# Where the weights of a sorted tile come from: a DRAM row loaded by SyncE instead of a copy by ScalarE

## The reference

```python
x = x + 0.5 * ffn(layernorm(x), Wg, bg, W1, b1, W2, b2)
x = x + attn(layernorm(x))
x = x + 0.5 * ffn(layernorm(x), Wg, bg, W1, b1, W2, b2)

def ffn(x, Wg, bg, W1, b1, W2, b2):          # 8 experts, the best 2 for each token
    probs = softmax(x @ Wg + bg)
    w, idx = top_k(probs, 2);  w = w / sum(w)
    h = relu(x @ W1[e] + b1[e])               # 128 -> 256, each expert e
    y = h @ W2[e] + b2[e]                     # 256 -> 128
    return sum over the two chosen e of w[e] * y[e]

def attn(x):                                  # 16 heads of 8 features
    c = x - mean(x over the tokens)
    return softmax(c @ c.T) @ x               # for each head
```

## Time and profile before

| | |
|---|---|
| median of 3 runs | 1019.24 us (1018.61 to 1019.99) |
| span of the profiled execution | 1039.1 us |
| TensorE busy | 975.9 us, 94% |
| ScalarE busy | 833.7 us, 80% |
| VectorE busy | 789.0 us, 76% |
| GpSimd busy | 529.3 us, 51% |
| ScalarE's `chosen<-weights` | 56 times, 59.2 us |
| DMA | 96.15 MB, mean 93 GB/s |

### The profile page before, as it was taken

How to read it: one execution, slowest core, us unless ns; L and a number is a source line. 1 busy time by engine, 2 the same in 40 slices (tenths; PEclk the granted TensorE clock), 3 DMA queues, 4 the chain that set the end, 5 groups by cost and what they waited for, 6 DMA issues and landing times.

```text
span 1039.1 us, 20329 instructions
## 1 busy us (share of the span) xinstructions
PE 975.9 (94%) x6512; PEld 546.9 (53%) x6512; DVE 789.0 (76%) x2255; ACT 833.7 (80%) x1194; POOL 529.3 (51%) x623
## 2 busy tenths in 40 slices
PE   7899999999999999989999999998999998888995
PEld 5687777633332488843333323332688862246673
DVE  5799999867767789857777777776878754368997
ACT  4655553599999988879999999998999988865653
POOL 5546777744444314354677766666100006555775
PEclk8999999999999999999999999999999999899998
DMA  6444223000051234420111111261444421133443
GB/s 182 165 152 133 100 102 103 14 21 20 19 147 60 75 130 163 145 89 24 36 37 35 36 37 34 57 179 36 122 139 146 143 83 49 44 127 107 131 155 121
DMA packets 59821, 96.15 MB, mean 93 GB/s; under 512 B 9179, under 2 KB 30403, under 8 KB 59715
## 3 DMA queue, kind: packets, MB, share of 16 engines
q1 hardware_dynamic: 47568, 71.50, 21.5%
q0 software_dynamic: 10752, 22.04, 7.1%
q10 hardware_dynamic: 1396, 1.31, 0.4%
HBM read 56.36 MB, written 38.45 MB: 91 GB/s over the span
## 4 chain that ended last, share of the span: by engine, by line
PE 53%; ACT 18%; issue 11%; DVE 10%; POOL 3%; DMA 3%; another core or an unknown queue 1%; SPq 0%; ACTq 0%; POOLq 0%; DVEq 0%
ACT probs L2023 10%; PE ps L1764 10%; PE ps L1749 6%; ACT sums L2023 5%; DVE low L1007 3%; PE ps L1375 3%; PE ps L1377 3%; PE ps L1376 2%; PE ps L1361 2%; PE ps L1386 2%; PE ps L1387 2%; PE ps L1391 2%; PE ps L1398 2%; PE ps L732 2%; PE ps L734 2%
## 5 line engine op out<-in xcount | busy, mean ns | idle before, releaser
L2023 ACT ACTIVATE probs<-ps 128x1024 f32<-128x1024 f32 x344 | 337.1, 1126 | 20.4 <-PE ps L1749 20.0
L1704 POOL DMA_INDIRECT found<-tiles,home x168 | 168.2, 1001 | 198.7 <-ACT sums L2023 126.9
L1692 POOL DMA_INDIRECT sorted<-xn,slot x168 | 168.1, 1000 | 179.2 <-ACT probs L2023 63.0
L1764 PE MATMUL ps<-probs,value 128*32 128x512 f32 x1376 | 185.2, 610 | 3.1 <-ACT probs L2023 1.4
L2023 ACT ACTIVATE sums<-ps 128x1024 f32<-128x1024 f32 x168 | 173.8, 1127 | 7.8 <-PE ps L1749 6.9
L1749 PE MATMUL ps<-shared 32*128 32x512 f16 x1024 | 144.7, 387 | 20.5 <-ACT probs L2023 6.8
L1188 ACT ACTIVATE high<-ps 128x512 fp32r<-128x512 f32 x176 | 101.1, 593 | 74.3 <-PE ps L734 58.7
L1007 DVE SCALAR_TENSOR_TENSOR low<-ps,high 128x512 fp32r<-128x512 f32 x176 | 113.0, 682 | 11.2 <-ACT high L1188 10.2
L1749 PEld LDWEIGHTS ps<-shared 32*128 32x128 f16 x1024 | 37.9, 91 | 157.8 <-ACT probs L2023 72.1
L1264 POOL TENSOR_TENSOR sums<-sums 128x512 f32<-128x512 f32 x59 | 76.6, 1298 | 66.6 <-DVE sums L1039 48.5
L1764 PE MATMUL ps<-sums,value 128*32 128x512 f32 x672 | 90.9, 613 | 0.2 <-ACT sums L2023 0.2
(11 more groups left out here) (202 smaller groups left out, 1869.2 us busy)
## 6 DMA issues: line engine op xcount, KB each, us to landing
found<-sorted SPq DMA_DIRECT2D x56, 256.0 KB
tiles<-sums SPq DMA_DIRECT2D x56, 256.0 KB
probs<-gates SPq DMA_DIRECT2D x24, 512.0 KB
wide<-gates SPq DMA_DIRECT2D x20, 512.0 KB
sorted<-zeros SPq DMA_DIRECT2D x16, 512.0 KB
out<-X SPq DMA_DIRECT2D x15, 256.0 KB
sorted<-xn,slot POOLq DMA_INDIRECT x168
found<-tiles,home POOLq DMA_INDIRECT x168
```

The costliest lines, as they stand in the source:

```text
L1692: nc.gpsimd.indirect_dma_start(sorted_rows[group_of(q)], bass.IndirectOffsetOnAxis(ap=slot[:, q % XNS, k, j:j + 1], axis=0), xn[:, rows_sl ...
L1704: nc.gpsimd.indirect_dma_start(found[:, q % 2, k, j, :], None, tile_rows[group_of(q)], bass.IndirectOffsetOnAxis(ap=home[:, q, k, j:j + 1] ...
L1764: ins = nc.tensor.matmul(ps[q * W:(q + 1) * W, MIX, :], value[:, s % 2, sd, j, m, q, :], ring[ring_at(g * UNITS + 2 * j + q // 2)][:, q % ...
L2023: nc.scalar.activation(ring[ring_at(n)], ps[:, score_banks(n), :], ACT.Exp, scale=SCORE).then_inc(sm["a_probs"], 1)
```

## The change

The split weights are written once to a new DRAM tensor `split` (8 experts x 128 x 1024 values, 4 MB), by one transfer that SyncE issues after the fourth later job's gates (n == 4), once all weights are made. ScalarE's copy `choose` is gone. In its place SyncE reads the number of the tile's expert from `expert_of` into a register and starts a transfer of 512 KB from the expert's row of `split` into the same place of `chosen` (`load_weights`). It waits for the same event as the copy did. `hidden(t)` waits for that transfer. ScalarE still needs the expert's number for the column of the bias, and reads it in `note_expert`, just before `biased`.

```diff
+            def load_weights(t):
+
+                y = tiles_of(t)
+                if t == 0:
+                    sp.wait_ge(sm["split_stored"], 16)
+                if t in TILE0:
+                    sp.wait_ge(sm["g_expert"], y + 1)
+                reached(sp, sm["t_expert"], t - 2)
+                of = nc.sync.value_load(expert_of[0:1, y, tile_at(t):tile_at(t) + 1], min_val=0, max_val=E - 1)
+                sp.dma_start(chosen[:, t % 3, :, :].rearrange("p k f -> p (k f)").bitcast(F32),
+                             split_dram[bass.ds(of, 1), :, :].rearrange("a p c -> p (a c)")).then_inc(weights_in[t % 3], 16)
...
             def sync_stream(a, b, at_slot):
                 for t in range(a, a + 2):
                     load_tile(t)
+                for t in range(a, a + 3):
+                    load_weights(t)
                 for i in stream(a, b):
+                    if i > a and in_stream(i + 2, a, b):
+                        load_weights(i + 2)
                     if in_stream(i + 4, a + 2, b):
                         load_tile(i + 4)
                     if in_stream(i - 2, a, b):
...
+                if n == 4:
+                    sp.dma_start(split_dram.rearrange("e p c -> p e c"),
+                                 weights[:, :, :, :].rearrange("p e k f -> p e (k f)").bitcast(F32)).then_inc(sm["split_stored"], 16)
...
             def hidden(t):
                 u = t % 2
-                pe.wait_ge(sm["t_weights"], t + 1)
+                pe.wait_ge(weights_in[t % 3], 16 * (t // 3 + 1))
...
-            def choose(t):
+            def note_expert(t):
                 if t in TILE0:
                     act.wait_ge(sm["g_expert"], tiles_of(t) + 1)
                 of[t] = nc.scalar.value_load(expert_of[0:1, tiles_of(t), tile_at(t):tile_at(t) + 1], min_val=0, max_val=E - 1)
-                reached(act, sm["t_expert"], t - 2)
-                nc.scalar.activation(chosen[:, t % 3, :, :].rearrange("p k f -> p (k f)"),
-                                     weights[:, bass.ds(of[t], 1), :, :].rearrange("p a k f -> p (a k f)"), ACT.Copy).then_inc(sm["t_weights"], 1)
...
             def biased(t):
+                note_expert(t)
```

More of the change, by code:

```diff
@@ L231, in third, with build @@
     return m % 3 if m < WHOLE * E else (m - WHOLE * E) % 3
-def build(nc, x_in, wg_in, bg_in, w1_rows, b1_in, w2_rows, b2_in, const_in, gates_dram, sorted_rows, tile_rows, out):
+def build(nc, x_in, wg_in, bg_in, w1_rows, b1_in, w2_rows, b2_in, const_in, split_dram, gates_dram, sorted_rows, tile_rows, out):
     with ExitStack() as ctx:
@@ L404, in build @@
         names = """const_in b1_in w1_in_0 w1_in_1 w1_in_2 w1_in_3 w2_in_0 w2_in_1 w2_in_2 w2_in_3 small_in stored value_set set_up wg_set b2_turned b2_set
- w1_shifted w1_high w1_low w2_high w2_low
+ split_stored w1_shifted w1_high w1_low w2_high w2_low
  f_mean f_rstd f_xn f_turned f_xnT f_xh f_xl f_logits f_logit_rows f_logits_turned f_lg f_ahead f_before
@@ L413, in build @@
  g_base g_zrowf g_zrow g_total g_count g_placed g_row g_home g_expert
- t_turned t_xh t_xl t_weights t_hidden t_high t_low t_expert t_y t_back t_out
+ t_turned t_xh t_xl t_hidden t_high t_low t_expert t_y t_back t_out
  c_half c_added
@@ L422, in build @@
         tile_in = sems("tile_in", 4)
+        weights_in = sems("weights_in", 3)
         tile_stored = sems("tile_stored", 2)
@@ L1668, in scalar_stream @@
                     x_high(i + 2)
-                if i == a - 2:
-                    choose(a)
-                    choose(a + 1)
                 if in_stream(i + 1, a, b):
                     relu(i + 1)
[L1674 to L1677, removed]
                 if i == b - 1:
@@ L2295 @@
     tile_rows = [nc.dram_tensor(f"tiles_{y}", ((TILE0[y + 1] - TILE0[y]) * T, D), F32, kind="Internal").ap() for y in range(2)]
-    build(nc, *args, gates_dram, sorted_rows, tile_rows, out)
+    split_dram = nc.dram_tensor("split", (E, P, 4 * F), F32, kind="Internal").ap()
+    build(nc, *args, split_dram, gates_dram, sorted_rows, tile_rows, out)
     return run(nc, [arrays], core_ids=[0]).results[0]["out"]
```

## The result

The changed kernel takes 1050.15 us (median of 4 runs, 1047.18 to 1053.78) against 1019.62 (1018.61 to 1020.1): ratio 1.0294 [1.0265, 1.0324], 30.5 us slower. I had said 1027.5, at most 1045. The direction and the place were right, the size was not.

A forecast was written before the change was run, and what follows sets the result against it. TensorE was taken to bound the kernel; 5.3 (late loads) + 1.5 (second stream's start) + 1.4 (gates) + 0.5 (store) - 0.4 (returns) = 8.3 us, added to 1019.24, gave 1027.5 us (own range 1022 to 1035; overall 1019 to 1045).

The forecast's parts named there:

- what bounds the kernel: Both tile streams: TensorE alone sets the pace, 3.68 us per plain tile, with ScalarE's copies beside it.
- what the copy was worth: Stream starts and last tile: removing ScalarE's copies returns at most 1.2 us, of which 0.4 survives late loads.
- the path: Tile streams: each load stands between tile t-3's expert matmuls and tile t's hidden matmuls, a stretch near 4.33 us.
- step (a): Weight load in the streams: from TensorE's event to the issue on SyncE, register load included, 0.75 us.
- step (b) + (c): Weight load, issue to TensorE: 3.03 us for the first 256 KB plus 0.82 us for 256 KB more.
- L: Total time from TensorE's event until the tile's weights are usable: 4.60 us, with ends 3.78 and 5.03.
- the streams' term: Loads late in both streams: 4.1 us in the second, 1.2 in the first, together 5.3 us; ends 0 and 14.
- Rival C: Streams: DMA engines become the bound, 4.4 to 4.9 us per tile; milder, L reaches 5.5; 1046 us, chance 0.15.
- My sign for it: Profile after, tile streams: a DMA share at 0.95 would show the DMA engines had become the bound.
- The start of the second stream: SyncE's queue: three weight loads ahead of tile load 2 delay the third tile, 1.5 us (0 to 2.5).
- The gates' wait: Mid second stream: SyncE waits for ScalarE's gates, so a weight load goes out 1.5 us late; cost 1.4 us, once.
- The store: Opening, about 117.3 us: the 4.2 MB split-weights store shares the engines with POOL's last send; cost 0.5 us.

## Why the prediction was wrong

**Right: what bounds the kernel and what the copy was worth.** ScalarE's copies lay beside TensorE; 49 us less of ScalarE bought at most the 1.7 to 2.5 us by which both streams together are shorter with four places and early weights. I had 0.4 surviving and 1.2 in all.

**Right: the path.** Expert event, register load, issue, transfer, hidden matmul.

**Half right: step (a), 0.75 us.** It measures 0.73 to 0.79 us in 23 of 50 tiles. In the other 27 it is up to 1.7 (2.07 behind the gates), 0.98 in the mean of all, mostly because the register read itself takes up to 0.99 us in place of 0.26. I had read (a) from one tile load of the kernel before, where no read is longer than 0.39 us. In the tiles that waited, this excess adds up to 6.7 us, so it is at most about a third of the streams' loss.

**Wrong: the transfer, step (b) + (c), 3.85 us.** I took the 3.03 us of tile 0 of the second stream, a load alone in an empty queue, and added only the new load's own second half. The loads of the stream are not alone: each follows a weight load, a tile load and a tile store, 1.05 MB per tile. Issue to landing as the chain has it in the second stream, with the time since the weight load before:

```
issued  751.38  768.32  784.82  794.65  807.04  823.45  840.68
gap       4.20    3.61    3.31    4.30    3.97    3.02    4.00
landed    4.69    5.01    5.60    4.58    5.18    5.47    5.45   us after issue
```

Within the second stream the two go together: 12 loads with a gap of 4.34 us or more landed in 3.2 to 3.8 us, 15 with less in 3.9 to 5.6. The gap is not the whole cause: in the first stream the same groups land in 3.4 to 5.8 and 3.5 to 5.6 us, and the slowest load of all (5.77) had a gap of 4.36. With (a) as it was in these seven tiles, L is 5.7 to 6.8 us for them, against my 4.60 with an upper end of 5.03. The loss per tile is 0.53 us in the second stream (16.0 / 30) instead of 0.15, and the streams' term, 5.3 us in the sum, measures 23.2 - 1.9 = 21.3 us. This is the mis-sized term; it alone is 16 us of the 22.6 by which the measured time is above the forecast. My upper end came from adding bytes to the quiet load. A bound for a queue with a whole tile's 1.05 MB in it would have been, as an estimate, 3.3 to 5.0 us of transfer at the 210 to 318 GB/s of the earlier trace rows, with the rest of the 3.03 us on top (3.03 - 0.262 / 210 = 1.8 us); the slowest landing measured is 5.8. The fit that the prediction quotes from the Trainium skill (DMA: Bandwidth & Descriptors, "Anatomy of one DMA — SWDGE (gpsimd) path") is stated there for GpSimd's transfers, while these loads are issued by SyncE; nothing in the sum hangs on it.

**Rival C was named and put too low.** Its strong form, DMA engines as the bound at 4.4 to 4.9 us per tile, is refuted: 275 GB/s with TensorE never idle. Its mild form, "loads that overlap stretch L to 5.5", is what happened, though not evenly: from the event to the hidden matmul it is 5.5 and 5.4 us in the mean of the two streams, made of tiles at 4.1 and tiles at 7.0. It gave 16 + 8 us in the streams and a total of 1046. I gave all of C 0.15 because I argued the case by throughput (the transfers fit in 3.6 us of 3.68), but traffic that fits, here at a DMA share of 0.79, can still make single loads land too late for a lead of 4.3 us. My sign for it, a share of 0.95, belonged to the strong form.

**The start of the second stream**, 1.5 us: 1.9 by the first three distances, 3.7 in the second trace.

**The gates' wait**, 1.4 us: the delay came and cost nothing. The gates go out at 789.26 and the load behind them at 790.35, 2.1 us after its event, but that tile is not late: the one before had been late already, and its hidden matmul stood at 790.47.

**The store**, 0.5 us: 1.9 by the times (interval 0.1 to 3.9), 0.1 to 1.9 at the send, by the medians 0.6. The argument for it was in part wrong: of the 4.4 us in which the send of the earlier trace rows moved no packet, about 1.6 are not the queue's doing, for a send at 207.18 us in the same trace, with no packet of q1 beside it, moves its first packet after 1.61 us as well.

**The sum by measured terms**, against the span of the kernel with the store alone: 7.2 (first stream) + 16.0 (second, its start included) + 3.5 (behind it) - 0.8 (ahead and between) = 25.9 us; in the second trace of the changed kernel 6.6 + 17.5 + 1.9 - 0.3 = 25.6. What the copies gave back is contained in the lengths. The 3.5 us behind the second stream cannot be put down to the change: that part is 173.8 to 177.6 us long in all traces but the first of before, 176.2 in its second and 176.3 with four places. Nothing is known of the cause of that spread, nor of the 4 us between the two timings of the changed kernel.

No version beats both kernels. The best, 1019.37 us, equals before: in the middle of the second stream TensorE is busy 99.91 of 100 us in before and 100.00 with four places, so there is hardly anything left for a load to give.

## What to carry over

When an on-chip copy is replaced by a load, its price is the lead between the event that frees its buffer and its first reader, against the landing time in the traffic that the stream will then have; a landing read from a quiet moment is a lower end. If all the bytes fit but with little to spare, ask for the data one tile earlier before doing anything about bytes: a place more took 20 to 24 us off here. Leaving out a quarter of the bytes took 20 to 25 where they were half of each late load, and 11 to 15 where they were other loads. Loads whose address is known early go ahead of the loads that wait for data.

## What the hardware showed that I had not expected

- One core's 16 DMA engines held 275 GB/s of mixed loads and stores at a share of 0.85 for 100 us without a late tile, while the single 512 KB loads in this stretch took 3.4 to 5.3 us, as far as their landing is known.
- The landing time of the same 512 KB load moved between 3.2 and 5.8 us within one kernel. In the second stream it was 3.2 to 3.8 us at a distance of 4.34 us or more from the weight load before, and 3.9 to 5.6 below; in the first stream the distance does not part them.
- The register read in front of a load took 0.26 us at best and up to 0.99 us, over 0.35 us in 25 of 50 tiles. With the tile stores issued by ScalarE it never took more than 0.30 us. The cause is open.
- A store of 4 MB in one DMA takes 0.56 us of SyncE and 18.5 us to land, and a send on POOL's queue passes beside it: 0.1 to 1.9 us later than without, 0.6 by the medians.
- A send on POOL's queue moved its first packet 1.6 us after its issue with q1 empty (207.18), and 4.4 to 4.7 us after it behind a full q1 (117.39 and 92.80).
